# Layer 1 of a four-layer kernel: where the second half of a batch's output product stands among the score parts of the next batch

## The reference

```python
xn = layernorm(x)
# branch 1: linear attention with a quadratic feature map, 16 heads of 16
q, k, v = heads(xn @ Wq.T), heads(xn @ Wk.T), heads(xn @ Wv.T)
phi_q, phi_k = feature_map(q), feature_map(k)   # normalised, scaled, shifted; all products of pairs
num = einsum('bhtf,bhtfd->bhtd', phi_q, cumsum(phi_k[..., :, None] * v[..., None, :], axis=2))
den = einsum('bhtf,bhtf->bht', phi_q, cumsum(phi_k, axis=2)) + EPS
y = num / den
# branch 2: product with a ternary weight
x = x + y @ Wo.T + (xn @ ternary_quantize(weight).T * alpha + bias)
```

## Time and profile before

| | |
|---|---|
| median of 3 runs | 3460.21 us (3457.18 to 3463.37) |
| profiled execution | 3464.72 us |
| its span, first to last instruction | 3463.0 us |
| TensorE, matmuls | 3044.8 us busy, 88% of the span |
| TensorE, weight loads | 1851.4 us, 53% |
| VectorE | 2107.1 us, 61% |
| ScalarE | 1393.6 us, 40% |
| GpSimd | 1390.0 us, 40% |

### The profile page before, as it was taken

The page is one execution under the profiler, slowest core; times in us unless marked ns, Lnnn a source line. Parts: engine busy times, 40 slices in busy tenths (PEclk is TensorE's granted clock), DMA queues, the critical chain, the costliest instruction groups (busy, mean ns, idle before and its releaser), DMA issues. The chain is left out here.

```text
span 3463.0 us, 46451 instructions
## 1 busy us (share of the span) xinstructions
PE 3044.8 (88%) x14629; PEld 1851.4 (53%) x14629; DVE 2107.1 (61%) x6568; ACT 1393.6 (40%) x3126; POOL 1390.0 (40%) x981
## 2 busy tenths in 40 slices
PE   7849995999699997999999998699999668898888
PEld 4427773666355554444444544565666445555554
DVE  4569998995544424466666654522222468888777
ACT  4425664453366652344343433122332323333331
POOL 1426100655244440122122212133005598988883
PEclk9879997999899998999999998789999879999999
DMA  5577553332300001000000000312223200000000
GB/s 186 180 253 227 177 153 110 110 110 73 126 1 1 1 1 43 7 19 7 13 19 19 19 13 13 131 57 84 92 84 92 80 0 7 7 7 7 7 7 13
DMA packets 138092, 221.08 MB, mean 64 GB/s; under 512 B 12800, under 2 KB 106240, under 8 KB 137088
## 3 DMA queue, kind: packets, MB, share of 16 engines
q1 hardware_dynamic: 99040, 146.92, 12.8%
q0 software_dynamic: 18432, 50.36, 4.6%
q10 hardware_dynamic: 20384, 20.84, 1.8%
HBM read 107.45 MB, written 110.62 MB: 63 GB/s over the span
## 5 line engine op out<-in xcount | busy, mean ns | idle before, releaser
L2313 DVE CUSTOM_DVE_ANT_0 a_ps_s<-a_ps_s,a_hide_row,a_fmax 128x384 f32<-128x384 f32 (+3 forms) x512 | 249.4, 555 | 170.3 <-PE a_ps_s L2020 170.1
L2225 POOL TENSOR_SCALAR_AFFINE_SELECT a_probs<-a_probs 128x512 f32<-128x512 f32 x128 | 79.7, 635 | 565.4 <-ACT a_probs L2502 565.4
L3594 POOL TENSOR_TENSOR c_prod<-c_att,c_v 128x2048 f32<-128x2048 f32 x64 | 287.3, 4529 | 29.1 <-DVE c_att L3654 29.1
L3594 POOL TENSOR_TENSOR c_prod<-c_q,c_k 128x2048 f32<-128x2048 f32 x64 | 286.5, 4508 | 16.5 <-ACT c_k L4005 13.5
L1521 POOL TENSOR_TENSOR a_probs<-a_probs,a_causal 128x512 f32<-128x512 f32 (+1 forms) x96 | 157.2, 1649 | 216.1 <-ACT a_probs L1750 216.1
L1750 ACT ACTIVATE a_probs<-a_ps_s 128x512 f32<-128x512 f32 (+1 forms) x384 | 170.7, 538 | 120.5 <-PE a_ps_s L1390 120.4
L2502 ACT ACTIVATE a_probs<-a_ps_s 128x512 f32<-128x512 f32 (+1 forms) x384 | 171.9, 538 | 91.1 <-PE a_ps_s L2042 90.5
L3428 PE MATMUL c_side<-c_w_e,c_h2T 128*128 128x512 f32 x448 | 203.4, 609 | 4.1 <-DVEq L3801 4.1
L703 PE MATMUL p_side<-p_w_expert,p_sortedT 128*128 x636 | 171.2, 392 | 0.0
L2881 POOL DMA_INDIRECT b_rows<-y_scratch,b_slot_int x64 | 62.7, 980 | 239.8 <-issue 239.8
L3654 DVE TENSOR_REDUCE c_att<-c_prod 128x128 f32<-128x2048 f32 x64 | 143.3, 2278 | 19.8 <-POOL c_prod L3594 18.0
(11 more groups left out here) (508 smaller groups left out, 7231.2 us busy)
## 6 DMA issues: line engine op xcount, KB each, us to landing
p_sorted_in<-sorted_scratch SPq DMA_DIRECT2D x39, 512.0 KB
y_scratch<-p_y_out SPq DMA_DIRECT2D x39, 512.0 KB
sorted_scratch<-all_zero ACTq DMA_DIRECT2D x1, 12160.0 KB, 57.8
sorted_scratch<-all_zero SPq DMA_DIRECT2D x1, 9088.0 KB, 30.7
b_sorted_in<-sorted_scratch SPq DMA_DIRECT2D x17, 512.0 KB, 4.5
y_scratch<-b_y_out SPq DMA_DIRECT2D x17, 512.0 KB, 3.2
sorted_scratch<-all_zero ACTq DMA_DIRECT2D x1, 8192.0 KB, 31.9
all_x_res<-x SPq DMA_DIRECT2D x8, 512.0 KB, 4.9
```

The source lines that it names most:

```text
L2313: last = nc.vector.tensor_tensor_reduce(out=there, in0=there, in1=hide_row[:, (TT - 1 - t) * P:], scale=HD ** -0.5, scalar=fmax[i % 2][:, ...
L3594: nc.gpsimd.tensor_tensor(out, left[:, heads].broadcast_to([P, HALF, HEADS, HD]), right.broadcast_to([P, HALF, HEADS, HD]), ALU.mult).then ...
```

## The change

In `slot3` of TensorE the second half of the output product of batch `i - 1` moves behind `score(i, 3, 1)`. It stood in front of it, and now stands between the last two score parts. No other engine's program is changed.

```diff
             def slot3(i, before, after):
                 score(i, 3, 0)
                 attend(i, 2)
+                score(i, 3, 1)
                 if before:
                     output(i - 1, 1)
-                score(i, 3, 1)
                 score(i, 3, 2)
                 if after:
                     turn_operand(i + 1, "k", D)
```

## The result

| | before | after |
|---|---|---|
| median of 10 runs each | 3461.97 us (3457.18 to 3466.67) | 3452.85 us (3446.39 to 3456.39) |
| ratio to before, 95% interval | | 0.9971 (0.9963 to 0.9980) |
| profiled execution | 3464.72 us | 3446.39 us |
| its span | 3463.0 us | 3444.7 us |

The change gains 0.29%, 10 us by the ratio. The forecast was 12 us less, 3448.2 us in a range of 3442 to 3456 us; the median is 4.7 us above the point, partly because the kernel before itself came out 1.8 us slower over ten runs than over the first three. The two profiled spans differ by 18.3 us, but the changed kernel's first score of layer 1 comes at 914.33 us, 4.4 us ahead of 918.75 us in the kernel before. Nothing up to there was touched, so that is the spread between runs. So the stage is compared by itself.

What follows compares the result with a forecast made beforehand. TensorE bounds layer 1, its last score part in slot 3 paced by ScalarE's squares. 9.4 + 2.5 = 11.9 us, taken as 12 off the 3460.2 us median, gives 3448.2 us, range 3442 to 3456 us.

Steps and rivals of the forecast that it cites:

- What bounds the stage: Layer 1, slot 3: the last score part goes at ScalarE's pace, most of its 2.10 us waiting booked as busy.
- The new border between attend and scores: Slot 3: score part 1 directly behind an attend waits 2.30 us, as output's 2.29 us does, so no cost.
- Score part 2: Slot 3: starts 4.75 us after the former output-half start (T), squares ready, and takes 0.65 us.
- The price of a batch: Slot 3, batches 1 to 6: fourth group of transposes comes 1.56 us earlier per batch, 9.4 us (8.8 to 13.0).
- What comes later: Slot 3: output half lands 1.10 us later; VectorE's output add, `normalise` and `late_keys` follow, at no cost.
- Batch 7, slot 3: The last attend waits for GpSimd's masks, which end earlier after the move; gain 2.5 us.
- The clock: Batches 1 to 6: two stretches at 0.86 lose 1.5 us; taken at zero, 1.5 us kept for the range.
- The first rival: Half clock in each of batches 1 to 6: gain shrinks to 4.9 us, 3455.3 us; chance 0.12.
- Sum: Layer 1: 9.4 us from batches 1 to 6 plus 2.5 us from batch 7, 11.9 us.
- the transposes' rule: Skill rule that full clock does not engage for transposes; by it all six stretches of batches 1 to 6 would fall.

Runs made afterwards that it cites:

- the split kernel: Against the kernel before, output half cut in two tiles of 128 rows, one before score part 1, one between parts 1 and 2; ratio 0.9957 (0.9942 to 0.9972).

## Why the prediction was right, step by step

- *What bounds the stage: right.* The loss sat in one place of slot 3, and TensorE's timeline showed it better than the list of waits. Moving one block took 1.68 us from each pass, with nothing given back in slots 0 to 2 of the next one.
- *The new border between attend and scores, at nothing: right.* The scores start 2.29 us after the attend, and part 1 holds TensorE 1.10 us.
- *Score part 2: right.* At T+4.75 and 0.64 us long, both as worked out. That the output half hides the squares is shown by the run with both parts in front of it, where the wait comes back.
- *The price of a batch: right, a little small.* 1.56 us were taken, 1.68 us measured. The term that was off is the start of the keys' read-out, put at T+6.69 and found at T+6.55: it starts 0.14 us before the record of the last square ends, 1092.49 against 1092.63, where no wait stands between them. The prediction named what would bound the place next, ScalarE's squares in front of the keys, and handing the keys to VectorE confirmed it with 0.53 us.
- *What comes later: right.* The output add starts at T+4.86, `late_keys` at T+6.75, and nobody waits for either. That `normalise` did not get longer is luck: it fell just between two of GpSimd's masks, which I had not looked at (below).
- *Batch 7, slot 3: right.* A gain of 2.5 us was expected for the mask; it ends at T+8.03 instead of T+10.55. The work behind the attend starts 2.85 us earlier. In the kernel before the attend lay at half clock (1291.5 to 1294.9), and after the change it doesn't, which I take for the rest.
- *The clock: taken at zero, and right by luck.* The two slow stretches of batches 1 to 6 did vanish, 1.5 us. The first rival, half clock in every batch through the longer wait and the transposes in a row, did not come in any. Instead the first two slots of batch 7 lost 3.0 us to half clock where they had lost 1.5 us, as the section on the hardware shows. Nothing in the prediction foresaw that the two would cancel.
- *Sum.* The six stretches give 6 times 1.68, which is 10.1 us, and 1.5 us for the clock there. Slot 3 of batch 7 gives 2.85 us and the rest of the stage 0.2 us; batch 7's first slots take 1.5 us back. That is 13.2 us for the stage, against 11.9 us on record. The whole kernel's ratios say 10.0 us (7 to 12.8) and 10.7 us (6.6 to 14.9). A stage gain of 12.7 to 13.2 us lies at the edge of the first interval and inside the second. Whether a microsecond or two is given back outside layer 1 stays open: outside it the two profiles of the kernel before took 3071.1 and 3063.0 us and those of the changed one 3066.0 and 3071.5 us, a spread larger than the question.

## What the runs showed of the hardware

**Where the clock falls.** In batches 1 to 6 half clock came only where a score part goes at ScalarE's pace. In four profiles of kernels that have it there (before twice, batch 7 only, behind both), 8 of 24 stretches lost 0.7 to 1.7 us to a lower granted clock. In eight profiles of kernels without it, none of 48 did. In all eight cases the clock fell 0.2 to 0.9 us after the end of the paced part, whatever stood behind it. With the output half behind both score parts, half clock lay on that half's matmuls alone: in batch 4 from 1146.35 to 1149.70, at a granted 0.50, with the first transpose at 1150.90. So the transposes' rule of the Trainium skill that was weighed above ("TensorE: Matmul & The Clock Gate", Part 4) was not the one at work: 30 of the 48 stretches without a loss hold 16 transposes between two score parts, with a wait of 0.75 to 1.16 us among them, and all ran at 1.00. That the paced part is the cause is an inference from these counts: 16 of 24 stretches that have it lost nothing.

Batch 7 has no side work in slot 0 and only the turning back in slot 1, and there the changed kernel was at half clock for longer. From attend to attend over two slots, these are the kernel before, then the changed one with its half-clock part, then the one with the move in batch 7 alone:

```profile
1252.60:1270.76 18.16, 17.45 (x148) 9.40 (x144) 3.34 (x12) 11.77 (x26) 9.72 (x6) 0.91 0.01 2
```

```profile
1236.45:1256.13 19.68, 18.97 (x148) 9.72 (x144) 2.96 (x12) 11.81 (x26) 8.80 (x6) 0.83 0.01 2
1242.50:1249.10 6.60, 6.60 (x37) 2.73 (x40) 0.00 (x0) 2.75 (x7) 4.39 (x3) 0.50 0.01 2
```

```profile
1252.36:1269.03 16.67, 15.96 (x149) 8.83 (x145) 2.97 (x12) 11.77 (x26) 8.85 (x6) 1.00 0.00 1
```

The same work takes 16.67 us at 1.00, 18.16 at 0.91 and 19.68 at 0.83. The second profiles of the first two kernels repeat it with 18.19 and 19.70 us. Yet the edit alone doesn't set where the clock falls. Up to slot 3 of batch 7 the third kernel has the very program of the kernel before; still it lost nothing here, and in batches 1 to 6 it fell in 1 and 5, where the kernel before fell in 1 and 4, twice. What decides the place was not tested.

**VectorE's normalisation is held up beside masks.** In the split kernel the four `normalise` instructions meet GpSimd's masks. This is VectorE in batch 3:

```profile
1094.36 4.01 DVE L121 TENSOR_SCALAR a_xn<-all_x_res,a_ln_moments,a_ln_rstd 128x256 f32<-128x256 f32 x4
```

And this is GpSimd, the part-1 mask and the shorter part-2 mask in one row:

```profile
1093.93 3.64 POOL L1526 TENSOR_TENSOR a_probs<-a_probs,a_causal 128x1024 f32<-128x1024 f32 x2 [3.97 <-ACT a_probs L1755]
```

They take 4.01 us, where they took 1.38 us with GpSimd idle. Taken one by one, the first lasts 2.08 us and ends 0.15 us after the part-1 mask, the second lasts 1.36 us and ends 0.16 us after the part-2 mask, and the last two take 0.4 us each, as without masks. So it looks like waiting for the end of a mask rather than a slower pace. In the changed kernel they run from T+5.46 to T+6.84 and still take 1.38 us, since the masks leave nearly that place free, T+5.66 to T+6.77. The Trainium skill ("GPSIMD Engine Reference", 1. Specifications) says that GpSimd shares its SBUF interfaces with VectorE, with contention when the VectorE instruction is in a 2-port performance mode or has two SBUF inputs. This case's trace agrees that there is contention, with 4.01 us for 1.38; in which mode these instructions run is not shown. Here the delayed key read-out had slack. My working for VectorE had not looked at GpSimd at all.

## What to carry to other kernels

A row of matmuls that a semaphore paces one by one is booked as busy, so compare starts with starts and with the same matmuls elsewhere: 2.09 us against 0.64 us showed 1.45 us of waiting, on top of the 0.65 us that the list of waits gave for the place. Work that fits between a producer and its next turn on the same banks belongs there, and it need not be longer than the other engine's turn: 1.83 us of it, beside squares of 2.06 us, gave 1.48 of 1.68 us. Then ask what is late next and weave the rest in by due time, which doubled the gain here; and on the way check what an instruction that moves will stand beside on the other engines: `normalise` beside masks took 4.01 us instead of 1.38.
